# Two peeled stages of a gated cross-attention and expert kernel written as loops over register values

## The reference

```python
def _L0_xattn_ref(q, c, wq, wk, wv):
    Q = einsum('bld,dh->blh', c, wq); K = einsum('bld,dh->blh', q, wk); V = einsum('bld,dh->blh', q, wv)
    attn = softmax(einsum('bch,bqh->bcq', Q, K), axis=2)
    return einsum('bcq,bqh->bch', attn, V)

def _L0_ffn_ref(x, Wg, W1, W2, W3):          # 8 experts, the 2 best of each token
    scores = xt @ Wg.T
    topk_scores, topk_idx = top_k(scores, 2)
    y = einsum('teh,edh->ted', silu(xt W1) * (xt W2), W3)
    return sum over the two experts of score * y

x = x + tanh(g_xattn[0]) * _L0_xattn_ref(ctx_1024, _layernorm(x), wq, wk, wv)
x = x + tanh(g_ffn[0]) * _L0_ffn_ref(_layernorm(x), Wg, W1, W2, W3)
```

## Time and profile before

| what | us |
|---|---|
| median of 3 runs | 611.57 |
| lowest, highest | 607.42, 613.79 |
| profiled execution | 611.57 |
| its span, first to last instruction | 609.8 |

### The profile page before, as it was taken

One profiled execution on the slowest core, in us unless ns is written; L12 is line 12 of the kernel. 1 busy time (PEld: TensorE's weight loads), 2 busy tenths in 40 slices (PEclk: granted clock), 3 DMA queues, 4 the chain that ended last, 5 costly groups with the idle time before them and its releaser, 6 DMA issues.

```text
span 609.8 us, 14365 instructions
## 1 busy us (share of the span) xinstructions
PE 553.5 (91%) x3947; PEld 418.7 (69%) x3948; DVE 293.4 (48%) x952; ACT 310.8 (51%) x502; POOL 255.4 (42%) x262
## 2 busy tenths in 40 slices
PE   4888988887877968998999999999999999999994
PEld 3776876776765646766777777777777777777772
DVE  1577677768786834433334333343334433344330
ACT  3988988988985422333333333333333333333331
POOL 4157777777774644332322233322332223322333
PEclk9999889999997989999999999999999999999997
DMA  7666676676451765887777776677767777667773
GB/s 229 198 194 212 206 223 207 210 242 221 160 174 60 154 123 106 138 137 119 120 114 115 118 121 113 110 118 116 120 111 113 120 115 119 114 108 124 116 110 56
DMA packets 191027, 86.63 MB, mean 142 GB/s; under 512 B 155408, under 2 KB 184848, under 8 KB 190992
## 3 DMA queue, kind: packets, MB, share of 16 engines
q1 hardware_dynamic: 173344, 63.76, 47.3%
q0 software_dynamic: 13296, 18.23, 18.3%
q10 hardware_dynamic: 4352, 4.20, 2.0%
HBM read 27.59 MB, written 23.66 MB: 84 GB/s over the span
## 4 chain that ended last, share of the span: by engine, by line
PE 57%; POOL 16%; SPq 7%; issue 6%; ACT 6%; DMA 5%; DVE 2%; another core or an unknown queue 0%; POOLq 0%; DVEq 0%; ACTq 0%
PE psum L855 36%; PE psum L905 18%; POOL rows_by_expert L510 6%; POOL xn2r L501 3%; POOL rstd L527 3%; ACT arena L580 3%; PE psum L752 2%; SPq L460 2%; SPq L452 2%; DMA w_in<-in_W2T 1%; POOL var_eps L524 1%; POOL neg_mean L525 1%; SPq L450 1%; DMA xa<-in_x 1%; SPq L435 1%
## 5 line engine op out<-in xcount | busy, mean ns | idle before, releaser
L855 PE MATMUL psum<-w_hi,arena 128*128 x1136 | 219.4, 316 | 8.3 <-DMA arena<-rows_by_expert 4.4
L561 POOL DMA_INDIRECT out<-arena,id_s x71 | 110.9, 1562 | 268.1 <-DMA out<-arena,id_s 157.8
L1192 DVE SCALAR_TENSOR_TENSOR arena<-psum,h_unit,arena 128x704 f32<-128x704 f32 x71 | 67.5, 951 | 189.4 <-PE psum L855 189.1
L855 PEld LDWEIGHTS psum<-w_hi,arena 128*128 128x128 f16 x1136 | 111.1, 99 | 65.0 <-issue 11.4
L855 PE MATMUL psum<-w_lo,arena 128*128 x568 | 132.7, 316 | 0.0
L698 ACT ACTIVATE arena<-arena 128x704 f16<-128x704 f32 x71 | 56.1, 790 | 145.5 <-DVE arena L1192 143.5
L692 ACT ACTIVATE arena<-psum,w_unscale 128x704 f32<-128x704 f32 x71 | 60.1, 847 | 105.1 <-PE psum L855 59.6
L905 PE MATMUL psum<-w_hi,arena 128*128 x781 | 110.1, 276 | 3.0 <-DMA arena<-arena 3.0
L905 PEld LDWEIGHTS psum<-w_hi,arena 128*128 128x128 f16 x781 | 77.0, 99 | 18.4 <-issue 3.2
L855 PEld LDWEIGHTS psum<-w_lo,arena 128*128 128x128 f16 x568 | 56.1, 99 | 30.1
L510 POOL DMA_INDIRECT rows_by_expert<-xn2r,slot_i x64 | 66.3, 1036 | 22.5 <-issue 16.9
(11 more groups left out here) (138 smaller groups left out, 557.8 us busy)
## 6 DMA issues: line engine op xcount, KB each, us to landing
w_in<-in_W1T SPq DMA_DIRECT2D x8, 704.0 KB, 4.2
w_in<-in_W2T SPq DMA_DIRECT2D x8, 704.0 KB, 4.2
w_in<-in_W3T SPq DMA_DIRECT2D x8, 640.0 KB
xa<-in_x SPq DMA_DIRECT2D x16, 256.0 KB
arena<-in_ctxT SPq DMA_DIRECT2D x16, 256.0 KB
out<-xa ACTq DMA_DIRECT2D x16, 256.0 KB
arena<-rows_by_expert SPq DMA_TRANSPOSE x71
meta<-rows_by_expert SPq DMA_DIRECT2D x71, 8.0 KB
```

The source lines that it names most:

```text
L561: pool.indirect_dma_start(out=out[:, :], out_offset=bass.IndirectOffsetOnAxis(ap=id_s[:, k4:k4 + 1], axis=0), in_=y_s[:, k, :], in_offset= ...
L855: ins = pe.matmul(ps[:, b, :], xg_t[:, k, x_part, c, :], w[w_part][:, c, bass.ds(e * H + b * HB, HB)], start=(q == 0 and c == 0), stop=(q ...
L1192: dve.scalar_tensor_tensor(out=hid, in0=u_ps, scalar=h_unit[:, 0, bass.ds(e, 1)].bitcast(F32), in1=act_g, op0=ALU.mult, op1=ALU.mult).then ...
```

## The change

`over_batches` peels only n = -2 to 3 and n = 14, 15. Steps 4 to 13 become a loop of five turns, two steps each, with n and i in registers. SP's steps 6 to 11 become a loop of three turns. `wait_alone` puts its wait for s_const ahead of constant values too. On PE, `rank` names its two waits in the other order, and the wait for s_half ahead of the router stands in front of the call instead of inside it. No operation on data is added, removed or put in another order.

```diff
         def wait_alone(eng, s, v):
-            if not isinstance(v, int):
-                v = eng.to_reg(v)
+            if not (isinstance(v, int) and v <= 0):
+                if not isinstance(v, int):
+                    v = eng.to_reg(v)
                 eng.wait_ge(s_const, CONSTS)
                 eng.wait_ge(s, v)
-            elif v > 0:
-                eng.wait_ge(s, v)
...
-            for n in range(-2, B):
+            for n in range(-2, 4):
+                peeled(n)
+            with eng.Fori(2, B // 2 - 1) as i:
+                for k in range(2):
+                    step(2 * i + k, i, k, lambda m: True)
+            for n in range(B - 2, B):
                 peeled(n)
...
-            for m in range(B):
+            for m in range(6):
+                step(m, m // 2, m % 2, lambda m: True)
+            with sp.Fori(3, B // 2 - 2) as i:
+                for k in range(2):
+                    step(2 * i + k, i, k, lambda m: True)
+            for m in range(B - 4, B):
                 step(m, m // 2, m % 2, lambda m: m < B)
...
             def rank(m, k):
+                pe.wait_ge(s_seen1, m + 1)
                 pe.wait_ge(s_rcopy, m + 1)
-                pe.wait_ge(s_seen1, m + 1)
...
-            def router(m, units=0):
+            def router(m):
                 pe.wait_ge(s_t2_copied, m + 1)
                 at_least(pe, s_place, m)
-                at_least(pe, s_half, units)
...
                 if on(n - 2) and not ending:
-                    router(n - 2, n + 1)
+                    pe.wait_ge(s_half, n + 1)
+                    router(n - 2)
```

More of the change, by code:

```diff
@@ L879, in moe_step @@
                     if at == 0:
-                        router(B - 3, B)
+                        pe.wait_ge(s_half, B)
+                        router(B - 3)
                         turn_probs(B - 1)
```

## The result

The changed kernel takes **630.04 us** (median of 4 runs, 628.72 to 631.30), the kernel before 610.59 (607.42 to 613.79) beside it: ratio 1.033, 95% interval 1.029 to 1.037. Forecast were 617.8 and a range of 610 to 626, so 19.4 us came where 6.2 were summed. The profiled execution took 632.62 us, of which the span is 630.6.

The account below looks back on a forecast made before the run. A ring of waits through POOL, ACT, PE and DVE was taken to set the batches' pace; 611.57 + 5.7 for register work in five pairs + 0.5 for entry gave 617.8 us, range 610 to 626.

Parts of the forecast that it names:

- The ring of shift, norms, router, DVE, rstd: Batch stage: the chain of waits each batch goes round; anything on it behind a wait is paid once a batch.
- PE's router answers; DVE's L1005 starts at 141.69 after an idle time that ends with the router: Link of the batch ring from PE to DVE: DVE's idle time was taken to end with the router.
- The sum, 5.7 us for five pairs: Looped batches: register work adds 0.58 us with k = 0 and 0.56 with k = 1, 1.14 a pair.
- 0.61 behind shift priced: ACT between shift and norms: waits and ISA instructions cost 0.38 us with k = 0 and 0.23 with k = 1.
- 0.48 priced: DVE from router to L948: 0.20 us in each step, plus 0.08 ahead of L954 with k = 1.
- The back edge: End of each loop turn on PE, DVE, ACT, POOL: 0.4 us, covered by other work; 0.5 us once on entry.
- The rival of 624.8 us: Back edge not covered: instructions fetched again, 1.4 us open per turn on POOL, 7 in all; chance 0.17.
- SP: SP's loop: eleven ISA per turn ahead of nine transfers, some 1.6 us spread over 22; cost nothing.
- The further wait for s_const, "nothing": The wait added ahead of constant values: costs nothing, since its value is reached at the start.
- The port turns: Rival: L954 delayed over 0.26 us lets POOL's rstd go first, saving 1.41 us a pair, 610.8 us; chance 0.10.

Follow-up runs that it names:

- e1: The changed kernel with one swap on DVE: the moments stand ahead of the MAX that waits for the router; 626.82 us, ratio 1.022.
- d1: The kernel before with the scatter's four DMA issues replaced by pow instructions on POOL and zero rows filled in afterwards; 718.93 us.
- d2: The changed kernel with the scatter's four DMA issues replaced by pow instructions on POOL and zero rows filled in afterwards; 729.33 us.
- b1: The changed kernel with POOL's batch stage written out again and its scatter waiting for the router's post s_rt; 659.6 us.
- c4: The kernel before with the first of four scatter issues ahead of the low rows, and the slots earlier on DVE; 614.8 us, ratio 1.004.

## Why the prediction was wrong

*What bounds the kernel.* The ring of shift, norms, router, DVE, rstd fits the traces. The stage of the experts stayed as it was: from the first L855 to the end 421.3 us before and 423.5 in the changed kernel, with 416 to 424 in the other runs. But **the step that failed** is in this part: "PE's router answers; DVE's L1005 starts at 141.69 after an idle time that ends with the router" took the idle time in front of MAX for PE's work. Of the 1.33 us at 131.14, 1.18 are a post held back, and the 0.47 in the earlier trace rows, on which I built, was the milder step of two (0.66 held). The ring has a term that belongs to no engine: the post behind its record's end, 1.0 us in the mean of a step before and 2.7 in the changed kernel (batches between 65 and 180 us). The sum has no term for it, and no price of an instruction could show it.

*The sum, 5.7 us for five pairs.* With no scatter in flight the five pairs cost 5.9, but that they agree is luck. At full clock a pair costs 0.62 there, which would be 3.1 in five, about half of what was summed; the rest came in two pairs in which PE ran at 1.2 GHz for a while. The sum had **no term for PE's clock** at all. By engine, with the scatter: ACT was priced well (0.52 a pair alone, 0.61 behind shift priced; 0.41 and 0.17 between s_rstd and s_xn2, for 0.38 and 0.23). DVE was not: 0.48 priced, 1.39 measured, of which 0.62 lie between s_rstd and s_xn2 of the k = 1 steps, where the view shows ACT waiting for a PE at the lower clock. What DVE's loop costs without the scatter, or at full clock, was not run.

*The back edge.* Covered, as forecast: POOL's loop costs 0.0 (22.74 us per pair against 22.75), PE's 0.01. The rival of 624.8 us has no part in it, although its time is the nearest.

*SP.* 1.8 us by the runs with an interval from -0.1 to 3.7, 0.12 a pair: small, as forecast.

*The further wait for s_const, "nothing".* Wrong where every step is peeled: 2.8 us together with the waits on PE (0.7 to 5.0), 0.39 a pair. I had looked at whether the value was reached, not at the instruction: it stands on the ring. In the changed kernel the edit acts on fewer steps, so its share there is smaller and was not measured.

*The port turns.* Neither turn as told. In the changed kernel's view rstd starts at 94.34, just behind the start of DVE's second L958 (94.18 to 95.13), and takes 1.69 us, and so it does in the other step, in place of 1.06 and 2.46. But in that other step shift takes 1.13 us instead of 0.20, and the stretch from L531 to the end of shift is 3.42 and 4.34 us, a little longer in a pair than before (3.1, and 4.4 in most k = 1 steps). Nothing was gained by it.

*The 19.4 us, as far as shown:* 10.4 without any flight, of which 5.9 lie in the looped batches, 3.1 of these in the pairs at the lower clock; 9.0 more with it. By e1, 3 us (its trace) to some 7 (its time) of the loss come by way of the moments behind MAX, so by the held post. That all of the 9.0 is the held posts' is argued, not shown, since d1 and d2 also shortened POOL's step. **Open** is why the loops of ACT and DVE together move the post from 3.7 to 4.4 and 5.8 us behind s_xn2. Each alone doesn't, plain delays on both don't, and PE's own program has no part in it. Open too is whether it is POOL's issuing or the rows' travel that holds the posts (every kernel here that took one away took both), and why they were not held in b1, beside a scatter. The clock, which seemed to mark b1, is ruled out.

## What to carry to other kernels

An idle time put down to an engine is that engine's work only if its last instruction ends there; subtract the two before you price a ring, and where semaphore times are to be had, look at the distance between two posts of one queue. Price the loop of a written-out program by engine: alone, POOL's, PE's and SP's cost 0.0 to 0.12 us a pair here, ACT's 0.52, and DVE's 1.39. The price of the instructions is not all: look in the trace whether the delays make PE idle and its clock fall, and count the pairs in which it does before you compare a sum with a measurement. A consumer that waits for a late post should stand behind everything in its queue that doesn't need it, but check what stands behind the consumer too: the swap alone gave back a third.

## What the runs showed of the hardware

Semaphore posts of PE can come late while POOL's indirect scatter (four issues of 128 rows, 1.3 us apart) is under way, and those of DVE, ACT and POOL did not (0.01 to 0.04 us behind their records' ends between 50 and 190 us, in every kernel here). A held post of the router rises 2.8, 3.5, 4.3 or 5.7 to 5.9 us after the scatter's first issue starts, at few other times, in every kernel in which the scatter was issued ahead of the router's end; z's follows at 5.7 to 5.9 in most steps, even where the record of its last matmul ends 1.7 us earlier. Loads and products go on meanwhile: v's post comes 0.01 to 0.11 us after its record's end. With the DMAs taken out all three rise 0.01 to 0.02 us after it. Beside a scatter they did so too in b1, at 1.2 GHz and at full clock, and z's in c4, where three issues stood behind the low rows and z ended 4.5 us or more after the first of them. PE's clock is not the cause: in the kernel before, the router's post was held for 1.22 us at 1.2 GHz.

PE's granted clock fell to 1.2 GHz once in every pair with DVE's loop alone, behind idle times of 1.4 and 1.9 us on PE. z then took 3.60 us instead of 1.97.
